# Closing stage of a Mamba and expert layer: TensorE adds the terms in PSUM, ScalarE copies out

## What is computed

```
out = x + LN_mamba(mamba(xn) + xn) * ln_g + ln_b
        + LN_ffn(experts(xn) + xn) * fln_g + fln_b
```

```
res = y @ W_out + b_out + x                       # x is xn here
res_norm = (res - mu) * rsqrt(var + LN_EPS) * ln_g + ln_b
...
out = jnp.einsum('ted,te->td', y, combine)
out = _ln(out + xf, ln_g, ln_b)
...
x = x + _L0_attn_ref(xn, ...) + _L0_ffn_ref(xn, ...)
```

## Time and profile before

| | us |
|---|---|
| median of 3 runs | 2136.91 (2131.9 to 2138.22) |
| the profiled execution, its own time | 2137.39 |
| its span, first to last instruction | 2135.6 |
| VectorE busy | 1866.7 (87%) |
| TensorE busy | 1636.0 (77%) |
| ScalarE busy | 1309.9 (61%) |
| GpSimd busy | 1066.6 (50%) |

### The profile page before, as it was taken

How to read it: one execution, slowest core, us unless ns; L and a number is a source line. 1 busy time by engine, 2 the same in 40 slices (tenths; PEclk the granted TensorE clock), 3 DMA queues, 4 the chain that set the end, 5 groups by cost and what they waited for, 6 DMA issues and landing times. The chain is left out here.

```text
span 2135.6 us, 27505 instructions
## 1 busy us (share of the span) xinstructions
PE 1636.0 (77%) x5288; PEld 862.2 (40%) x5289; DVE 1866.7 (87%) x2815; ACT 1309.9 (61%) x2119; POOL 1066.6 (50%) x885
## 2 busy tenths in 40 slices
PE   4673899999999999999999999999999998300000
PEld 4551445454444444454444444454444545100000
DVE  6766799899989999898989889899989994399999
ACT  3431576767767676776767676767676673333333
POOL 3777444444444444444444444444444441477775
PEclk9996899999999999999999999999999999755555
DMA  7945222222222222222222222212222221344443
GB/s 210 340 161 211 69 76 70 85 79 72 77 74 75 88 75 70 84 71 79 75 69 79 84 74 79 77 62 89 74 74 79 72 77 58 103 141 149 154 149 120
DMA packets 144220, 213.93 MB, mean 100 GB/s; under 512 B 26470, under 2 KB 112358, under 8 KB 144121
## 3 DMA queue, kind: packets, MB, share of 16 engines
q1 hardware_dynamic: 126988, 170.96, 24.6%
q0 software_dynamic: 12288, 33.57, 4.7%
q10 hardware_dynamic: 4848, 8.56, 1.2%
HBM read 148.21 MB, written 64.82 MB: 100 GB/s over the span
## 5 line engine op out<-in xcount | busy, mean ns | idle before, releaser
L481 POOL TENSOR_TENSOR area<-area,more 128x1024 f32<-128x1024 f32 x258 | 608.0, 2357 | 700.2 <-DVE area L1059 700.2
L593 ACT ACTIVATE area<-area,A_sb 128x512 f32<-128x512 f32 x516 | 343.7, 714 | 271.3 <-DVE area L1059 271.0
L824 PE MATMUL psY<-area,ident 128*128 128x512 f32 x1032 | 490.4, 620 | 0.0
L1059 DVE TENSOR_TENSOR_SCAN area<-area 128x512 f32<-128x512 f32 x256 | 326.1, 1334 | 48.8 <-ACT area L593 17.8
L1059 DVE TENSOR_TENSOR_SCAN area<-area,h_last 128x512 f32<-128x512 f32 x256 | 345.4, 1408 | 14.0 <-PE psY L824 13.7
L1075 DVE TENSOR_TENSOR area<-area,psC 128x1024 f32<-128x1024 f32 x256 | 308.4, 1205 | 16.7 <-DVE hstats L1080 13.7
L797 PE MATMUL psH<-w_sb,ffn_xT 128*128 x556 | 267.9, 604 | 39.4 <-DVE h_norm L1089 34.4
L824 PEld LDWEIGHTS psY<-area,ident 128*128 128x128 f32 x1032 | 197.0, 200 | 209.5 <-issue 209.5
L807 PE MATMUL psX<-w_sb,h_T 128*128 x1024 | 256.1, 393 | 1.5 <-issue 1.5
L615 ACT ACTIVATE h_T<-psT,be_T,g_T 128x128 f32<-128x128 f32 x552 | 207.9, 457 | 6.2 <-issue 4.6
L807 PEld LDWEIGHTS psX<-w_sb,h_T 128*128 128x128 f32 x1024 | 184.7, 190 | 51.4 <-issue 31.3
(11 more groups left out here) (176 smaller groups left out, 2394.7 us busy)
## 6 DMA issues: line engine op xcount, KB each, us to landing
more<-B_rows_d SPq DMA_DIRECT2D x130, 512.0 KB, 3.8
xin<-sorted_x SPq DMA_DIRECT2D x140, 128.0 KB, 2.0
sorted_y<-y_out SPq DMA_DIRECT2D x138, 128.0 KB, 1.9
area<-xnT_d SPq DMA_DIRECT2D x18, 512.0 KB
mamba_d<-mo_stage SPq DMA_DIRECT2D x17, 512.0 KB, 2.8
area<-L_attn_x SPq DMA_DIRECT2D x8, 1024.0 KB, 6.1
xnT_d<-w_sb ACTq DMA_DIRECT2D x16, 512.0 KB, 3.3
w_sb<-L_ffn_w SPq DMA_DIRECT2D x16, 512.0 KB
```

Source lines behind the costliest of these rows:

```text
L481: pool.tensor_tensor(inflow[:, k], dtx, B_rep[par][:, k].rearrange("p (a t) -> p a t", a=1).to_broadcast([P, KD, CHUNK]), ALU.mult).then_i ...
L593: e = nc.scalar.activation(decay[:, k, hd], dt_sb[par][:, hd], ACT.Exp, scale=A_sb[:, hd, n:n + 1])
L824: m = nc.tensor.matmul(psY[:, hd * CHUNK:(hd + 1) * CHUNK], ident[:, :], h_sb[:, 2 * before + k, hd], start=False, stop=True, skip_group_c ...
L1059: a = V.tensor_tensor_scan(h_sb[:, buf, hd], decay[:, k, hd], inflow[:, k, hd], start, ALU.mult, ALU.add)
```

## The change

- GpSimd only gathers; its two additions are gone.
- VectorE makes `er0` as ex * rstd + emo (two instructions). That leaves out -mean * rstd, the same number for a whole row, which the layer norm that follows takes away again. `exn` is ex * rstd likewise, by ScalarE without a bias, and `shift` is gone. VectorE's two final sums are gone; it ends a pair with the two gain products, which signal `e_gain`.
- TensorE adds up in PSUM (one half of psY for even pairs, one for odd): identity times x, a row of ones times the bias row (two halves), identity times `er0`, identity times `er1`. Then it signals `e_sum`.
- ScalarE copies the sum from PSUM to `eo` and signals `e_done`. In its queue the copy of pair p-1 stands behind the root of p+1, the scaled x of p+2 and the normalised sums of p.
- TensorE waits for `e_done` of pair p-2 before it writes its half of psY.

```diff
@@ gpsimd, behind the four gathers of a pair
-                pool.wait_ge(S[f"ex_in{q}"], 32 * (k + 1))
-                pool.wait_ge(S[f"e_store{q}"], 16 * k + 16)
-                pool.tensor_tensor(eo[q], ex[q], e_b0.rearrange("p (o d) -> p o d", o=1).to_broadcast([P, 2, DIM]), ALU.add
-                                   ).then_inc(S["e_xb"], 1)
-                pool.wait_ge(S["exn_ready"], u + 1)
-                pool.tensor_tensor(er0[q], emo[q], exn[q], ALU.add).then_inc(S["e_mamba"], 1)
@@ scalar
-                    a = nc.scalar.activation(exn[q][:, t, :], ex[q][:, t, :], ACT.Identity, scale=rstd[:, at], bias=shift[:, at])
+                    a = nc.scalar.activation(exn[q][:, t, :], ex[q][:, t, :], ACT.Copy, scale=rstd[:, at])
+            def copy_out(k, off):
+
+                q, n = off % END_BUFS, k + off // END_BUFS
+                act.wait_ge(S["e_sum"], k * END_BUFS + off + 1)
+                act.wait_ge(S[f"e_store{q}"], 16 * n + 16)
+                nc.scalar.activation(eo[q], psY[:, q % 2 * CHUNK:(q % 2 + 1) * CHUNK].rearrange("p (t d) -> p t d", t=2), ACT.Copy
+                                     ).then_inc(S[f"e_done{q}"], 1)
             with act.Fori(0, (PAIRS_E - END_BUFS) // END_BUFS) as k:
-                for q in range(END_BUFS):
+                for q in range(1, END_BUFS + 1):
                     root(k, q + 1)
-                    normalise_x(k, q + 2)
+                    scale_x(k, q + 2)
                     normalise_sums(k, q)
+                    copy_out(k, q - 1)
@@ tensor
+            with pe.Fori(0, TILES // 2 // END_BUFS) as k:
+                for q in range(END_BUFS):
+                    total = psY[:, q % 2 * CHUNK:(q % 2 + 1) * CHUNK]
+                    pe.wait_ge(S[f"e_done{(q + 2) % END_BUFS}"], k + 1 + q // 2)
+                    pe.wait_ge(S[f"ex_in{q}"], 32 * (k + 1))
+                    nc.tensor.matmul(total, ident[:, :], ex[q].rearrange("p t d -> p (t d)"), start=True, stop=False)
+                    for t in range(2):
+                        nc.tensor.matmul(total[:, t * DIM:(t + 1) * DIM], ones[0:1, :], e_b0[0:1, :], start=False, stop=False)
+                    pe.wait_ge(S["e_gain"], k * END_BUFS + q + 1)
+                    nc.tensor.matmul(total, ident[:, :], er0[q].rearrange("p t d -> p (t d)"), start=False, stop=False)
+                    nc.tensor.matmul(total, ident[:, :], er1[q].rearrange("p t d -> p (t d)"), start=False, stop=True
+                                     ).then_inc(S["e_sum"], 1)
@@ vector, sums
-                dve.wait_ge(S["e_mamba"], k * END_BUFS + off + 1)
-                dve.wait_ge(S[f"ey_in{q}"], 64 * (n + 1))
+                dve.wait_ge(S[f"ex_in{q}"], 32 * (n + 1))
+                for t in range(2):
+                    e_chain.mark(V.scalar_tensor_tensor(er0[q][:, t, :], ex[q][:, t, :], rstd[:, bass.ds(tile + t, 1)],
+                                                        emo[q][:, t, :], ALU.mult, ALU.add))
+                dve.wait_ge(S["exn_ready"], p + 1)
+                dve.wait_ge(S[f"ey_in{q}"], 64 * (n + 1))
...
@@ vector, result becomes gains
-                    e_chain.mark(V.tensor_tensor(v[q], v[q], two(gain), ALU.mult))
-                e_chain.wait()
-                e_chain.mark(V.tensor_tensor(er0[q], er0[q], er1[q], ALU.add))
-                dve.wait_ge(S["e_xb"], p + 1)
-                e_chain.wait()
-                V.tensor_tensor(eo[q], eo[q], er0[q], ALU.add).then_inc(S[f"e_done{q}"], 1)
+                    a = V.tensor_tensor(v[q], v[q], two(gain), ALU.mult)
+                a.then_inc(S["e_gain"], 1)
```

More of the change, by code:

```diff
@@ L244, in build_program @@
             y_ready y_copied y_stored pool_consts
-            e_bias e_xb e_mamba exn_ready e_chain e_var e_sqrt e_scale e_norm""".split()
+            e_bias exn_ready e_chain e_var e_sqrt e_scale e_norm e_gain e_sum""".split()
         names += [f"{n}{q}" for n in ("ex_in", "ey_in", "e_done", "e_store") for q in range(END_BUFS)]
@@ L682, in _, with scale_x @@
                 gelu(u, expert(u))
[L685 removed]
+            def scale_x(k, off):
                 q, n = off % END_BUFS, k + off // END_BUFS
@@ L706, in normalise_sums @@
                 a.then_inc(S["e_norm"], 1)
+            def copy_out(k, off):
[4 more added lines that the diff above has]
+                                     ).then_inc(S[f"e_done{q}"], 1)
             PAIRS_E = TILES // 2
-            normalise_x(0, 0)
-            normalise_x(0, 1)
+            scale_x(0, 0)
+            scale_x(0, 1)
             root(0, 0)
+            root(0, 1)
+            scale_x(0, 2)
+            normalise_sums(0, 0)
             with act.Fori(0, (PAIRS_E - END_BUFS) // END_BUFS) as k:
-                for q in range(END_BUFS):
+                for q in range(1, END_BUFS + 1):
                     root(k, q + 1)
-                    normalise_x(k, q + 2)
+                    scale_x(k, q + 2)
                     normalise_sums(k, q)
-            for p in range(PAIRS_E - END_BUFS, PAIRS_E):
+                    copy_out(k, q - 1)
+            for p in range(PAIRS_E - END_BUFS + 1, PAIRS_E + 1):
                 if p + 1 < PAIRS_E:
@@ L1280, in sums @@
                 q, n = off % END_BUFS, k + off // END_BUFS
-                tile = (k * END_BUFS + off) * 2
-                dve.wait_ge(S["e_mamba"], k * END_BUFS + off + 1)
-                dve.wait_ge(S[f"ey_in{q}"], 64 * (n + 1))
[L1284 to L1287, removed]
-                    e_chain.wait()
-                for l, v in enumerate((er0, er1)):
-                    for t in range(2):
-                        e_chain.mark(V.bn_stats(estats[q][:, t, l, :], v[q][:, t, :]))
+                p = k * END_BUFS + off
+                tile = p * 2
+                dve.wait_ge(S[f"ex_in{q}"], 32 * (n + 1))
[3 more added lines that the diff above has]
+                dve.wait_ge(S["exn_ready"], p + 1)
+                dve.wait_ge(S[f"ey_in{q}"], 64 * (n + 1))
+                for t in range(2):
+                    e_chain.mark(V.scalar_tensor_tensor(er1[q][:, t, :], ey1[q][:, t, :], weight[:, bass.ds(tile + t, 1), 0],
+                                                        exn[q][:, t, :], ALU.mult, ALU.add))
+                e_chain.wait()
+                for t in range(2):
+                    e_chain.mark(V.scalar_tensor_tensor(er1[q][:, t, :], ey2[q][:, t, :], weight[:, bass.ds(tile + t, 1), 1],
+                                                        er1[q][:, t, :], ALU.mult, ALU.add))
+                for t in range(2):
+                    e_chain.mark(V.bn_stats(estats[q][:, t, 0, :], er0[q][:, t, :]))
+                e_chain.wait()
+                for t in range(2):
+                    e_chain.mark(V.bn_stats(estats[q][:, t, 1, :], er1[q][:, t, :]))
                 e_chain.wait()
@@ L1327, in _ @@
                         sums(k, q + 2)
-                        result(k, q)
+                        gains(k, q)
             for p in range(PAIRS_E - END_BUFS, PAIRS_E):
@@ L1333, in _ @@
                     sums(0, p + 2)
-                result(0, p)
+                gains(0, p)
 _INS = ['L0_attn_x', 'L0_attn_W_in', 'L0_attn_b_in', 'L0_attn_conv_w', 'L0_attn_conv_b', 'L0_attn_W_bc', 'L0_attn_b_bc',
```

18 lines of the change are left out of this document (9 added, 9 removed).

## The result

The changed kernel takes 2122.62 us (median of 6 runs, 2117.51 to 2125.39) against 2136.81 for the kernel before (6 runs beside it, 2131.88 to 2140.21). The ratio is 0.9936, with a 95% interval of 0.9922 to 0.9951. The profiled execution has a span of 2120.0 us, 15.6 less than before.

What follows compares the result with a forecast made beforehand. VectorE bounds the kernel at 8.77 us a pair; after the change a ring through load and ScalarE takes 8.79. 1868.8 + 28 x 8.79 = 2114.9, plus 18.1, 2.6 and 1.8 gives 2137.4, stated as 2138; range 2126 to 2149.

Steps and rivals of the forecast that it cites:

- VectorE's stretch: Closing stage: VectorE's L1313 and L1316 each lose some 0.95 us beside GpSimd's own two adds.
- new sum: VectorE's work for one pair after the change: 6.44 us, against 8.79 a pair before.
- The ring: Closing stage, e_done to next e_done: load 5.17, scaling 0.95, normalising 1.98, wait and copy 0.69; 8.79 us a pair.
- the scaling: ScalarE's two x scalings of a pair without bias: 0.88 to 1.00 us, taken as 0.95.
- the copy: ScalarE's new copy out of PSUM: 0.51 to 0.71 us, taken as 0.62, plus 0.07 for its wait on two semaphores.
- the load's landing: From e_done to ScalarE's start on the loaded data: 4.90 to 5.59 us, mean 5.17.
- The range: Whole kernel: 2126 to 2149 us, from 0.25 either way on the ring over 28 pairs and 4.5 on TensorE's end.
- Start and end: Closing stage: e_done(0) at 1868.8, 4.7 us earlier than before; after e_done(28) 18.1 us (13.6 to 22.6), against 13.25 before.
- TensorE beside the ring: TensorE's low clock, with products of 7.2 us a pair, lies beside the ring; ScalarE waiting for e_sum would disprove it.
- the ring over two pairs: Closing stage, through gathers, adds, gains, TensorE and copy: 16.6 us, or 8.3 a pair; 7.4 with TensorE at full clock.
- the 0.3% that I had called no change: Whole kernel: a difference of 6.4 us counts as none; faster 0.24, same 0.50, slower 0.26.
- The rival's 2122: Faster by a little: ring of 8.39 us a pair and TensorE at full clock at the end, 2122 us; chance 0.20.

Runs made afterwards that it cites:

- b1: Kernel before, with GpSimd's two additions of a pair replaced by their signals alone, so its output lacks these terms; 52.7 us less.
- e4_again: Second run of the changed kernel with loads and gathers of pair p+4 no longer waiting for e_done(p); 2054.28 against 2134.01 us, ratio 0.9620.
- e5: Changed kernel with the bias of the x scaling and the shift back; 2132.41 us against 2127.77 for the changed kernel run again.
- e2: Changed kernel, but GpSimd gathers for pair p+4 once the sums of pair p are made, not after e_done(p); ratio 0.991, 7.93 us a pair.
- e1: Changed kernel, but ScalarE copies out pair p-1 ahead of normalising pair p; 8.38 us a pair, 280.8 us from first gather to last copy.
- e0_again: The changed kernel run once more, unedited, against the kernel before; 2127.77 against 2134.91 us, ratio 0.9949.
- e2_again: Second run of the changed kernel with gathers released by the sums of pair p instead of e_done(p); 2115.62 against 2134.01 us, ratio 0.9906.

## Why the prediction was wrong

- **VectorE's stretch and its new sum.** Right that the adds stretched it (b1), and that it would not stay the bound. The sum of 6.44 was 0.3 too high: in e4_again the pair is 6.13.
- **The ring.** The path was right link by link: the timeline shows it, e5 shows that ScalarE lies on it (0.17 us a pair for 0.19), e2 that the load does. Its size was the step that failed. I had 5.17 + 0.95 + 1.98 + 0.69 = 8.79; measured 5.06 + 0.81 + 1.97 + 0.57 = 8.41 in an undisturbed pair, and 8.45 in the mean, with the few copies that come late. The largest miss is the scaling: without its bias it takes 500 ns and 0.81 for two, below my lower bound of 0.88. For that bound I had named an exponential over 512 columns with a scale alone and a normalisation over 256 with a bias, and worked nothing out from them. (The Trainium skill, ScalarE: Activation LUTs, "What ACT_TABLE_LOAD costs", says that each per-partition operand column adds about 93 ns; the 593 and 500 of the two kernels agree, and I had not drawn on it. By that figure, as an estimate, two scalings without the bias would have been priced 0.19 below the 1.00.) Next the copy: 0.57 in all, under the 0.58 of its lower bound with the wait, and the wait for two semaphores, priced at 0.07, cost nothing (1.97 from normalising to copy has it in). Then 0.11 of the load's landing. All erred the same way, and I had treated them as if they would cancel. From copy 0 to copy 28 it took 236.5 us instead of 246.1, 9.6 less.
- **The range.** It was built from 0.25 a pair either way, 8.54 to 9.04; the terms' own lower bounds gave 8.39 and 2122, and the range should have begun there.
- **Start and end.** First gather to copy 0: 26.9 predicted, 26.5 measured. From copy 28 to the last 18.1 predicted, 16.9 measured. The rows of the end:

```profile
2099.93 0.57 ACT L705 ACTIVATE area<-psY 128x512 f32<-128x512 f32 x1
...
2104.24 2.08 PE L941 MATMUL psY<-area,ident 128*128 128x512 f32 x2 [2.59 <-DVE area L1339]
...
2106.11 1.92 PE L942 MATMUL psY<-area,ident 128*128 128x512 f32 x2
...
2110.93 1.13 PE L941 MATMUL psY<-area,ident 128*128 128x512 f32 x2
...
2116.78 0.60 ACT L705 ACTIVATE area<-psY 128x512 f32<-128x512 f32 x1 [3.23 <-PE psY L942]
```

  TensorE starts at 2104.24 at the low clock (2.08 for one product) and is at the full one at 2110.93 (1.13), so half of each, as I had taken it. From 2104.24 to its last product 12.5 us, against 13.5.
- **TensorE beside the ring.** Right, narrowly: 6 copies wait for it, 11.1 us in all, and three of these are the end (2.75, 2.34 and 3.23 at 2108.06, 2112.95 and 2116.78). e1 shows that its products, as a link of the ring over two pairs, set the pace once the other ring is shorter.
- **The rest.** 4.4 us of the 15.6 between the two traces lie in stages that the change leaves alone; e0_again shows them as spread between executions. So the 15.6 are 4.4 of spread, 0.4 at the start, 9.6 in the ring and 1.2 at the end. The forecast had been put 0.6 above its own sum as well, for a copy that might cost more. Without the 4.4 the measured ratio is 0.995, as in e0_again, still outside the 0.3% that I had called no change. The median of e0_again, 2127.77, would have been inside my range, so the miss is narrow.
- **The rival's 2122 is partly luck.** Its ring of 8.39 came close to 8.45, with a landing that was too short (4.95 for 5.06) and a scaling that was too long (0.88 for 0.81). But it took 4.5 us off the end, where 1.2 came, and knew nothing of the 4.4 us of spread, which made up for that.
- **A misreading.** The clock row falls to half in the last five slices, not the last eight; no term hangs on it.

## What to carry to other kernels

When an edit relieves the busiest engine, follow the buffer's release, not the engine's sum: with few buffers, whoever signals "free" stands in a ring with the transfers that this lets start, and moving that signal behind two more engines can cost what the edit won. Release each buffer by its last reader (here two semaphores and one more wait of VectorE, and 80 us instead of 14), and cut all rings of similar length at once: here the gathers alone brought 16 us more in the stage, the loads alone cost 8, and both together brought 71. And where the forecast is one short ring times 28, take the bounds of every link into the range before adding them up: small links that are priced by a neighbour's instruction err in the same direction.

## What the runs showed of the hardware

- VectorE's two-input add over 128x512 from SBUF takes 0.69 us alone, and beside GpSimd's own adds mostly 1.64 and up to 3.25; gathers of GpSimd do not stretch it (671 ns for L1339 beside them, 692 for L1312 in b1). The Trainium skill (SBUF — State Buffer, "SBUF: two separate sides") says that the first of the two engines on their shared port pair blocks the other for its whole instruction; b1, in which the stretch is gone with GpSimd's adds, agrees.
- ScalarE over 128x256 from SBUF: 585 to 593 ns with a scale and a bias column, 500 with a scale alone; 128x512 out of PSUM without either, 574 in the median and 571 to 597.
- A one-row fp32 product costs its columns and is no cheaper for its single row: two over 256 columns take 1.13 us at the full clock (L939 at 2113.71), as much as a 128x512 one over all rows (1.13, L941 at 2110.93).
- In the steady part of the changed kernel TensorE was busy for 70% of the time, in bursts, and its mean granted clock was 0.69; in e4_again it was busy for 78% and the clock was 0.83. The idle time just ahead of a burst does not tell its clock: behind 2.59 us of idle a product took 2.08 us (2104.24), behind 1.79 in e2_again also 2.08 (at 2008.50), and behind 2.15 in e4_again 1.12 (at 1959.16).
- From a copy's end to ScalarE's start on the loaded data it takes 5.06 us with the gathers issued ahead of the loads, and 4.6 to 4.7 with the loads issued first (e2_gather_early and e2_again). The order is the difference that the timelines show; it was not tried by itself.
